# Cross-attention and routed experts: natural scores in 32-row tiles, batched by three, with the period's order dealt anew

## What is computed

```python
# x (4,1024,256), ctx (4,77,256), mask (4,77); 16 heads of 16; 8 experts, FF 1024
q, k, v = heads(layernorm(x) @ Wq.T + bq), heads(ctx @ Wk.T + bk), heads(ctx @ Wv.T + bv)
s = where(mask, -inf, q @ k.T / sqrt(16))
x = x + (softmax(s) @ v) @ Wo.T + bo
t = layernorm(x);  probs = softmax(t @ Wr);  idx, pmax = argmax(probs), max(probs)
# a token goes to its expert's next free slot, as long as that has any (640 each)
y = relu(t @ W1[idx]) @ W2[idx]  if kept, else t
x = x + y * (pmax if kept else 1)
```

## Time and profile before

| | us |
|---|---|
| median of 3 runs | 485.07 |
| lowest, highest | 483.9, 486.75 |
| span of the profiled execution, first to last instruction | 484.0 |
| TensorE busy | 450.2 |
| VectorE, GpSimd, ScalarE busy | 208.3, 189.0, 143.9 |

### The profile page before, as it was taken

One profiled execution on the slowest core, in us unless ns is written; L12 is line 12 of the kernel. 1 busy time (PEld: TensorE's weight loads), 2 busy tenths in 40 slices (PEclk: granted clock), 3 DMA queues, 4 the chain that ended last, 5 costly groups with the idle time before them and its releaser, 6 DMA issues.

```text
span 484.0 us, 10848 instructions
## 1 busy us (share of the span) xinstructions
PE 450.2 (93%) x4347; PEld 293.2 (61%) x4348; DVE 208.3 (43%) x612; ACT 143.9 (30%) x208; POOL 189.0 (39%) x328
## 2 busy tenths in 40 slices
PE   7997989899999999979489999999999999999995
PEld 3442424233333333324238899899899899989894
DVE  5877445758583847555813221221211311313210
ACT  1233555545555563655203110010010010111000
POOL 5753370857877372946651411011011012121212
PEclk9999999999999999999989999999999999999999
DMA  7899845442435342534052610610610612443000
GB/s 205 255 243 214 238 140 184 160 137 88 148 112 167 96 164 88 180 102 141 35 147 83 208 62 23 211 54 23 219 36 22 230 35 89 171 168 106 7 23 12
DMA packets 49960, 60.82 MB, mean 126 GB/s; under 512 B 4802, under 2 KB 40617, under 8 KB 49904
## 3 DMA queue, kind: packets, MB, share of 16 engines
q1 hardware_dynamic: 42224, 47.49, 32.3%
q0 software_dynamic: 3456, 7.35, 4.4%
q10 hardware_dynamic: 4224, 5.21, 3.7%
HBM read 31.79 MB, written 26.62 MB: 121 GB/s over the span
## 4 chain that ended last, share of the span: by engine, by line
PE 77%; DVE 12%; issue 4%; DMA 4%; ACT 2%; POOL 1%; ACTq 0%; DVEq 0%; POOLq 0%
PE tps L1773 11%; PE wk L1783 11%; PE tps L1793 11%; PE wk L1801 11%; PE wk L1522 6%; PE nat L1470 6%; PE wk L1573 5%; PE wk L1399 3%; DMA sums<-shared 3%; PE tps L1495 2%; DVE rowmax L980 2%; PE nat L1811 2%; DVE bn L1061 1%; DVE attn_mem L1009 1%; DMA mask_u<-in_mask 1%
## 5 line engine op out<-in xcount | busy, mean ns | idle before, releaser
L708 POOL DMA_INDIRECT out_x<-attn_mem,dest x40 | 39.0, 976 | 183.9 <-DVE attn_mem L1304 181.2
L747 ACT ACTIVATE shared<-tps,mask_key 77x1024 f32<-77x1024 f32 x64 | 68.2, 1105 | 38.2 <-PE tps L1495 38.2
L980 DVE TENSOR_REDUCE rowmax<-nat 128x8 f32<-128x616 f32 x58 | 46.0, 794 | 34.9 <-PE nat L1470 34.8
L1783 PE MATMUL wk<-w_sb,shared 128*128 128x256 f32 x256 | 57.7, 379 | 0.0
L1773 PE MATMUL tps<-shared,w_sb 128*128 128x256 f32 x256 | 56.6, 379 | 0.8 <-ACT shared L851 0.8
L1793 PEld LDWEIGHTS tps<-shared,w_sb 128*128 128x128 f32 x480 | 56.0, 192 | 0.8
L1793 PE MATMUL tps<-shared,w_sb 128*128 128x128 f32 x480 | 56.0, 275 | 0.0
L1801 PE MATMUL wk<-w_sb,shared 128*128 128x256 f32 x240 | 54.3, 379 | 0.0
L1773 PEld LDWEIGHTS tps<-shared,w_sb 128*128 128x128 f32 x256 | 48.6, 190 | 7.5 <-issue 1.0
L1783 PEld LDWEIGHTS wk<-w_sb,shared 128*128 128x128 f32 x256 | 48.0, 190 | 6.2
L1470 PE MATMUL nat<-kblk,qT 64*32 64x308 f32 x928 | 43.9, 430 | 8.1 <-DVE rowmax L980 7.2
(11 more groups left out here) (211 smaller groups left out, 521.8 us busy)
## 6 DMA issues: line engine op xcount, KB each, us to landing
w_sb<-in_w SPq DMA_DIRECT2D x12, 1024.0 KB, 8.4
strips<-shared SPq DMA_DIRECT2D x28, 256.0 KB, 2.6
slot_rows<-zeros SPq DMA_DIRECT2D x1, 5340.0 KB, 32.6
x_sb<-slot_rows SPq DMA_DIRECT2D x7, 667.5 KB, 4.3
x_sb<-in_x SPq DMA_DIRECT2D x8, 512.0 KB, 9.0
w_sb<-in_w ACTq DMA_DIRECT2D x4, 1024.0 KB, 9.7
out_x<-base SPq DMA_DIRECT2D x8, 512.0 KB
attn_mem<-strips SPq DMA_DIRECT2D x28, 128.0 KB
```

The lines of the kernel that those rows point to most:

```text
L708: pool.indirect_dma_start(out_rows, bass.IndirectOffsetOnAxis(ap=dest[n % 2][:, c:c + 1], axis=0), y_sb[n % 2][:, c, :], None, bounds_chec ...
L747: act.activation(probsT[0:SK, r % 2, 2 * i:2 * i + 2, :], tps[0:SK, 2 * i:2 * i + 2, :], ACT.Exp, bias=mask_key[:, g // GPB:g // GPB + 1]) ...
L980: dve.tensor_reduce(rowmax[:, j, :, m, :], nat_heads(g, i), AX.X, ALU.max).then_inc(rowmax_ready, 1)
L1783: last = pe.matmul(wk[(SC * n + c) % 2][:, 0:D], hidden[:, f, c * P:(c + 1) * P], w2_sb[n % 2][:, f, :], start=(f == 0), stop=(f == FC - 1))
```

## The change

Natural scores are made in tiles of 32 rows (two heads) by 128 columns (tokens). A call is four products that move 2 x 77 = 154 columns, one for each quarter of the rows, and each into a bank of its own: two in `tps`, two in `nat`. Three batches a period take 3, 3 and 2 calls side by side in the banks; a batch waits for the first half of the exponentials that frees `tps`, and the next scores wait for the batch's maximum over `tps`. Each batch has two maxima (one for each pair of banks). The group 0 keeps the old calls. The transposition of the normalised rows moves to group a and to the period's start; the second and third use of `wk` banks are dealt anew, with both halves of a projection in `wk[1]`. From group 4 on, VectorE normalises two of four tiles. GpSimd's normalising comes ahead of bias and dispatch.

```diff
+NORM_SPLIT = 2
+CALLS = KD * TPG
-NAT_ORDER = (0, 2, 4, 6, 1, 3, 5, 7)
+NAT_BATCHES = ((0, 3), (3, 6), (6, 8))
+        def nat_part(part):
+            return nat[:, :, :] if part else tps[:, 0:2, :]
         def projected(g, h):
             if g < LAST - 1:
-                return wk[h]
+                return wk[1]
...
             def first_norm(g):                                   # GpSimd
...
-                for j in range(TPG):
+                for j in range(NORM_SPLIT if g >= EARLY else TPG):
...
                 if has(c):
+                    if has(l) and l >= EARLY:
+                        first_rstd(l)
+                        first_norm(l)
                     add_output_bias(c, n if c == 0 else None)
-                    if has(m):
-                        first_rstd(m)
...
                     dispatch(o)
-                if has(c) and has(m):
-                    first_norm(m)
...
                     exponentials(c, 0)                           # ScalarE
+                    if c > 0 and has(a):
+                        copy_xnT(a)
                     bias_query(n, 1)
+                    if c == 0:
+                        copy_xnT(a)
                     exponentials(c, 1)
...
                     copy_attn(c, 1)
-                    exponentials(c, 3, (0,))
                     if has(r):
                         bias_logits(r)
-                    exponentials(c, 3, (1,))
+                    exponentials(c, 3)
                     if c < 2:
                         load_weights(c)
                     copy_attn(c, 2)
+                    copy_maxT(n)
                     copy_attn(c, 3)
-                    copy_maxT(n)
-                    if has(l):
-                        copy_xnT(l)
...
+            def rest_of_norm(g):                                 # VectorE
+                wait(dve, rstd1_ready, g + 1)
+                wait(dve, xnT_ps, KD * g)
+                for j in range(NORM_SPLIT, TPG):
+                    last = dve.tensor_scalar(xn[:, j:j + 1, :], x_sb[:, group(g, j, 1), :], mv1[:, j, 0:1], rstd1[:, j:j + 1],
+                                             ALU.subtract, ALU.mult)
+                last.then_inc(xn_rest_ready, 1)
+            def row_maxima(g, b, part):
+                at, end = NAT_BATCHES[b]
+                wait(dve, nat_ps, nat_filled(g, b))
+                dve.tensor_reduce(rowmax[:, 2 * part:2 * part + 2, at:end, :].rearrange("p q i r -> p q (i r)"),
+                                  nat_part(part)[:, :, 0:(end - at) * 2 * SK].rearrange("p q (n k) -> p q n k", k=SK),
+                                  AX.X, ALU.max).then_inc(rowmax_ready, 1)
...
                 if has(c):                                       # VectorE's new order, c > 0
+                    if has(o):
+                        masked_positions(o)
...
+                    elif has(a):
+                        copy_xnT(a)
                     if has(r):
                         invert_sums(r)
+                    row_maxima(n, 0, 0)
+                    row_maxima(n, 0, 1)
                     if has(o):
                         place(o)
                     if has(a):
                         copy_u(a)
+                    row_maxima(n, 1, 0)
+                    row_maxima(n, 1, 1)
+                    if has(l) and l >= EARLY:
+                        rest_of_norm(l)
                     if has(r):
                         normalise_attn(r)
+                    row_maxima(n, 2, 0)
+                    row_maxima(n, 2, 1)
                     if has(r):
                         add_residual(r, 0)
                     split_maxima(n)
                     if has(r):
                         add_residual(r, 1)
                         take_logits(r)
                         choose(r)
                         second_stats(r, 0)
                         second_stats(r, 1)
                         second_moments(r)
+                    if has(m):
+                        first_moments(m)
...
             def transpose_xn(g, k):                              # TensorE
                 wait(pe, xn_ready, g + 1)
+                wait(pe, xn_rest_ready, g - EARLY + 1)
...
+                elif k == 1:
+                    wait(pe, attnU_ready, ROUNDS * (g - 3) + 3)
+                else:
                     wait(pe, attnU_ready, ROUNDS * (g - 2))
+                    wait(pe, posm_ready, g - 3)
...
+            def natural_scores(g, b):
+                batch = g // GPB
+                at, end = NAT_BATCHES[b]
+                wait(pe, q_ready, KD * g + (end - 1) // TPG + 1)
+                wait(pe, probsT_ready, 2 * (ROUNDS * (g - 1) + b) + 1)
+                if b > 0:
+                    wait(pe, rowmax_ready, maxima_taken(g, b - 1, 1))
...
+                for i in range(at, end):
+                    j, m = i % TPG, i // TPG
+                    for q in range(4):
+                        of = slice(q * QUARTER, (q + 1) * QUARTER)
+                        last = pe.matmul(nat_part(q // 2)[:, q % 2, (i - at) * 2 * SK:(i - at + 1) * 2 * SK],
+                                         qT[g % 2][of, m, j * P:(j + 1) * P],
+                                         kblk[of, batch, m, (q % 2) * 2:(q % 2) * 2 + 2, :].rearrange("p r k -> p (r k)"),
+                                         start=True, stop=True)
                 last.then_inc(nat_ps, 1)
...
             def scores(g, r):
...
+                elif g < LAST:
+                    wait(pe, rowmax_ready, maxima_taken(g + 1, r - 1, 0))
```

More of the change, by code:

```diff
@@ L574, in add_output_bias @@
                 for j in range(TPG):
-                    if has(n):
-                        wait(pool, nat_ps, 2 * TPG * n + j + 3)
+                    if has(n) and j < len(NAT_BATCHES):
+                        wait(pool, nat_ps, nat_filled(n, j))
                     last = pool.tensor_tensor(x_sb[:, group(g, j, 1), :], x_sb[:, group(g, j, 1), :], bo_sb[:, None, :], ALU.add)
@@ L956, in first_moments @@
                 wait(dve, xn_ready, g)
+                wait(dve, xn_rest_ready, g - EARLY)
                 for j in range(TPG):
@@ L982, in split_maxima @@
             def split_maxima(g):
-                flat = rowmax[:, :, :, :, :].rearrange("p t g m r -> p (t g) (m r)")
-                rest = rest1[:, :, :, :, :].rearrange("p t g m r -> p (t g) (m r)")
-                parts = max_nat[:, :, :].rearrange("p t (g c) -> p (t g) c", g=4)
-                hi, mid, low = (parts[:, :, i * ROUNDS:(i + 1) * ROUNDS] for i in range(PIECES))
-                wait(dve, rowmax_ready, 2 * TPG * (g + 1))
+                flat = rowmax[:, :, :, :].rearrange("p q (m t) r -> p t (q m) r", m=KD)
@@ L989, in split_maxima @@
+                rest = rest1[:, :, :, :].rearrange("p q (m t) r -> p t (q m) r", m=KD)
+                parts = max_nat[:, :, :].rearrange("p t (w c) -> p t w c", w=4 * KD)
+                hi, mid, low = (parts[:, :, :, 2 * i:2 * i + 2] for i in range(PIECES))
+                wait(dve, rowmax_ready, CALLS if g == 0 else maxima_taken(g, len(NAT_BATCHES) - 1, 1))
                 wait(dve, maxT_ps, g)
@@ new lines, in first_natural_scores @@
+                last.then_inc(nat_ps, 1)
+            def natural_scores(g, b):
+                batch = g // GPB
+                at, end = NAT_BATCHES[b]
+                wait(pe, q_ready, KD * g + (end - 1) // TPG + 1)
+                wait(pe, kblk_ready, KD * batch + KD)
+                wait(pe, probsT_ready, 2 * (ROUNDS * (g - 1) + b) + 1)
+                if b > 0:
+                    wait(pe, rowmax_ready, maxima_taken(g, b - 1, 1))
+                else:
+                    if g == 1:
+                        wait(pe, v_ready, B)
+                    wait(pe, maxT_ready, g)
+                    wait(pe, logits_ready, g - 2)
+                for i in range(at, end):
+                    j, m = i % TPG, i // TPG
+                    for q in range(4):
[4 more added lines that the diff above has]
+                                         start=True, stop=True)
@@ L1516, in weigh_values @@
                     else:
-                        wait(pe, x1_ready, 2 * (g - 1) + 1)
+                        wait(pe, lgT_ready, g)
+                else:
+                    if g == 0:
+                        wait(pe, wowr_ready, 2)
+                    else:
+                        wait(pe, x1_ready, 2 * g)
                 wait(pe, probsT_ready, 2 * (ROUNDS * g + r) + 2)
@@ L1692, in step @@
                         transpose_output_weights()
-                    natural_scores(n, 7)
+                    scores(c, 3)
                     if has(r):
                         project(r, 1, c)
-                    weigh_values(c, 3)
-                    if not has(r):
-                        router_products()
+                    weigh_values(c, 2)
                     transpose_maxima(n)
@@ L1702, in step @@
                         transpose_logits(r)
-                    if has(l):
```

(5 more changed lines are left out.)

211 lines of the change are left out of this document (90 added, 121 removed).

## The result

The changed kernel takes 497.01 us (median of 4 runs, 495.45 to 498.01) beside 484.88 of the kernel before (4 runs, 483.9 to 486.75): a ratio of 1.0232 with an interval of 1.0193 to 1.0272. It is slower by 12 us, where 480.4 was forecast, in a range that ended at 488. Some executions of a kernel come out slower at a lower granted clock; a ratio compares runs of one state, as far as they can be told apart, so it can differ from the quotient of the two medians. The profiled execution is the longest of the four: 498.01 us, 1.0 above the median, with a span of 496.3.

What follows compares the result with a forecast made beforehand. TensorE bounds by its amount of work, 24.07 of 25.24 us in a steady period. Changes of -3.6 (c = 0), +3.2 (1, 2), -1.3 (3, 4), -2.4 (5), -0.8 (6) take 484.0 to 479.3, 480.4 as median; range 472 to 488.

Steps and rivals of the forecast that it cites:

- the price of the natural scores: TensorE's natural batches: 0.94 us for three calls, 0.68 for two, 2.56 a period in place of 5.44.
- Rival (c): Natural batches: each pass waits for its own weights, giving 487.5 us, or 501 with load and pass in line; chance 0.12.
- the 21.2 that was worked out: TensorE's work in a steady period: falls from 24.07 to 21.2 us.
- The rest of the steady period: Steady periods: 24.6 us for c = 3 and 4 instead of 25.24; 22.8 after periods without first moments.
- where the stall goes: Period's start: TensorE waits 2.6 us for masked positions behind VectorE's first moments, ahead of the second transposition.
- On the queue of SyncE nothing is issued anew: SyncE's queue: gathers, stores and eight spreading transfers keep their order; only what releases them moves.
- what follows (last group, experts) has unchanged order: After period 6: the last group and experts keep their order, with no change in time counted.
- the clock: Period c = 1: one clock fall counted behind TensorE's idle, 3.8 x 0.47 = 1.8 us.
- rival (d): Heads of periods: the clock falls at each, 1.8 x 3 or 4 us more, 486.5 us; chance 0.13.
- the sums at c = 1 and 2: Periods 1 and 2: second scores wait for late-landing sums, at 10.5 and 9.4 us; periods 27.2 and 26.1.
- the two norm tiles that were priced at 2 x 0.41 us: VectorE: third and fourth norm tiles add 2 x 0.41 us, its sum hardly changing.

Runs made afterwards that it cites:

- e3_gathers: Kernel after, with SyncE's gather of the round 3 sums issued ahead of the stores of rounds 2 and 3 and round 1's packing: 487.93 us, ratio 1.0014.
- e2_moments: Kernel after, with first moments of periods 1 to 3 moved from VectorE's end of period to behind the attention's normalising: 494.33 us, ratio 1.0159.
- e1_fill: Kernel after, with idle products put where TensorE waits, in periods 1 to 4: 495.05 us, ratio 1.0152.
- e4_invert: Kernel after, with the reciprocal of the sums behind the first two maxima in periods 1 and 2: 498.32 us, ratio 1.0232.
- e5_weights: Kernel after, with the first two experts' weights loaded behind the first attention copy of periods 1 and 2: 494.86 us, ratio 1.0127.
- e9_loads_apart: Kernel after, with first moments moved, last gather early, four 1 MB weight loads each behind the second attention copy of periods 1 to 4: 475.08 us, ratio 0.9749.
- e8_bias: Kernel after, with first moments moved, last gather early, weights loaded later, and GpSimd's bias behind its dispatch: 491.28 us, ratio 1.0057.

## Why the prediction was wrong

**Right: the price of the natural scores.** Batches of 1.00 and 0.73 us (132.21 to 132.94) for 0.94 and 0.68, passes 0.13 apart beside weight loads of 206 ns mean, one for every pass (the half of them that goes into `tps`, in the groups up to 260 us):

```profile
L1518 PE MATMUL tps<-kblk,qT 32*128 32x154 f32 x224 | 22.8, 335 | 4.3 <-ACT shared L763 3.3 <-issue 1.0
L1518 PEld LDWEIGHTS tps<-kblk,qT 32*128 32x128 f32 x224 | 17.9, 206 | 15.0 <-issue 15.0
```

Rival (c), by which each pass waits for its weights, is refuted. The Trainium skill, TensorE: Matmul & The Clock Gate, Part 3, The mechanism, says that a load overlaps only with products of another row group. These rows do not agree with it: each row tile has a load of 206 ns for every pass, and its passes follow every 0.13 us. TensorE's work without a fall, 21.9 to 22.1 us in e3_gathers, stands above the 21.2 that was worked out, by more than the 0.2 us of the three batches; where the other 0.5 to 0.7 lies is open. The rest of the steady period, 24.8 for 24.6 and 22.9 for 22.6, holds.

**Right: where the stall goes.** 2.17 us for masked positions, for 2.6; e2_moments brings it to 0.5.

**Wrong, and the largest: "On the queue of SyncE nothing is issued anew; its gathers, stores and eight spreading transfers keep their order, but what releases them moves".** The sentence saw that the releases move, but the landing was worked out for c = 1 and 2 alone, behind the weights' loading; for every later group it was put at nothing. The released gather falls behind a store of 256 KB, and lands 3.7 to 3.9 us after its issue instead of 1.7 to 1.8. Nothing covers these 2 us: the reciprocal waits for them in periods 5 and 6 (1.72 and 2.13 us), ahead of the first maximum, where the change had put it, and the slots behind it run into GpSimd's bias. e3_gathers prices the step, with the falls that went with it: 1.0232 to 1.0014, some 10 us. Undone, it leaves 487.93 us, at the upper end of the range and not at 480.4: it is the largest single step, not the only one.

**Wrong as well: "what follows (last group, experts) has unchanged order".** The order is unchanged; its input, the normalised attention of the group before, comes 2.7 us later. The queue's order is the smaller part of this: in e3_gathers the normalising starts 218.78 - 205.59 = 13.2 us after the rest's beginning, for 13.8 after the change and 11.1 before, and the rest still takes 277.2. Why the reciprocals are spread late there stays open.

**Wrong in number: the clock.** One fall within the periods was counted, at 1.8 us (for 3.8 us of work at half clock; the whole fall that it was read from lasted 6.8, 239.95 to 246.78 before); rival (d) had three or four more and a chance of 0.13. In the profiled execution it fell at 65.0, 92.3, 119.6, 146.9 and 204.9 us within the periods, and twice in the rest. One of 3.4 us at half clock costs 1.44 in a steady period (e1_fill, e4_invert). Rival (d) was thus right in kind for c = 2, 3 and 4, each with a fall behind its 2.17 us for masked positions: at c = 3 and 4 these make nearly all of the 3.3 us, at c = 2 the 1.1. It had none for period 6, where one came behind a wait of 2.03 us for a maximum. Which wait brings a fall, the runs don't settle: the same wait of period 3 stood without one in e3_gathers and e4_invert.

**Right but for the clock: the sums at c = 1 and 2.** The landings, 7.0 and 6.5 us, were worked out at 7.6 and 6.5, so the waits are as forecast; period 1 exceeds its 29.0 where the fall was longer (10.2 us at half, not 3.8), period 2 its 26.1 where one was not counted (at 92.3). That the late landings go with the loading of weights, as the forecast said, e5_weights and e9_loads_apart show.

**Not seen: GpSimd's bias beside VectorE's instructions** (below): the slots in periods 5 and 6, and the two norm tiles that were priced at 2 x 0.41 us, which took 1.56 in period 3 (129.86), beside the bias.

The answer "faster" was therefore right of the arithmetic that was changed, and wrong of the schedule that came with it. The range failed because it was built from prices of instructions: the one queue whose releases moved had been given no price behind period 2, not even an upper end, and no rival put late sums and falls of the clock together.

## What to carry to other kernels

A queue that keeps its order is not unchanged when its releases come closer together: for each small transfer that someone waits for, write down what is issued on its queue within the two or three us ahead of it, and issue it first. A load that is needed much later is best cut into parts that fit between such transfers, and its new place has its own victims. When an engine's work shrinks, price each wait that appears at its head twice, as the wait and as a possible fall of the granted clock behind it, and give the range a case in which every one of them falls.

## What the runs showed of the hardware that was not expected

An instruction of VectorE on 128 x 4 numbers can take 2.85 us. In period 5 of the kernel after:

```profile
175.73 2.85 DVE L1145 TENSOR_SCALAR past<-pos 128x4 f32<-128x4 f32 x1
175.77 2.78 POOL L594 TENSOR_TENSOR x_sb<-x_sb,bo_sb 128x256 f32<-128x256 f32 x4
...
178.50 0.15 DVE L1146 TENSOR_TENSOR slotf<-first,pos 128x4 f32<-128x4 f32 x1
...
179.26 1.06 PE L1434 MATMUL wk<-xnT,wq_sb 128*32 128x512 f32 x8 [1.46 <-DVE uT L1050]
```

It ends with the four bias additions of GpSimd (175.77 + 2.78), not after the first of them, and the query behind it waited 1.46 us. In period 6 four instructions of the slots took 0.66 to 0.79 us each beside the additions instead. In period 3 a maximum of L1010 runs beside the additions at its usual 1.1 us (128.84), and in e8_bias the normalising was held up, as told above. The stall of the slots stands in the kernel after and in e1_fill, e2_moments, e4_invert and e5_weights, where the sums of period 5 land late, and in no run with the gathers early, where the slots are done before the bias starts. The Trainium skill, SBUF — State Buffer, Who interferes with whom, says that VectorE and GpSimd share a pair of ports, held by one of them for a whole instruction, that a VectorE instruction with two inputs in SBUF or in a two-port mode contends for it, and that a reduction never does. These rows agree with that on which instructions stall; that the stall lasts over four instructions of GpSimd in a row, the section doesn't say.

A second surprise is how far the granted clock of one kernel's executions lies apart: 0.958 to 0.982 in ten runs of e3_gathers (484.6 to 495.4 us), beside 0.977 to 0.991 in thirteen of the kernel before on the same chip (486.3 to 494.7). That the many short waits are the reason was not tested.
